# A new order of the same pieces on four engines, in a fused kernel of RWKV, a gated recurrence and two mixture-of-experts passes

## The chip, the cores and the metric

The kernel runs on one core of one Trainium2 chip. A core has five engines that each run their own list of instructions in order: TensorE (PE in the profile; PEld are its weight loads), VectorE (DVE), ScalarE (ACT), GpSimd (POOL) and SyncE (SP), which here only issues DMAs. They wait for each other through semaphores. The metric is the device time of one execution in microseconds; lower is better. Before the change it is 1342.73 us, the median of three runs (1339.48 to 1346.77).

## What is computed

The input `x` has 16 sequences of 512 tokens with 256 features. Four residual blocks follow one another, and each sees the layer-normalized rows of the one before:

```
x = x + attn_a(layernorm(x))     # RWKV: time mix with WKV scan, then channel mix
x = x + ffn(layernorm(x))        # mixture of experts
x = x + attn_b(layernorm(x))     # convolution, gates, linear recurrence, RMS norm
x = x + ffn(layernorm(x))        # mixture of experts, the same weights

# attn_a, per sequence
k, v, r = (mix of xn and its shifted rows) @ w_key, w_value, w_recept
x = x + wkv(exp(time_decay), time_first, k, v) * sigmoid(r) @ w_output
fk, fr = (mix of layernorm(x) and its shifted rows) @ f_w_key (256 x 1024), f_w_recept
x = x + sigmoid(fr) * (relu(fk) ** 2 @ f_w_value)
# attn_b, per sequence
c = depthwise_conv(x, 4 taps);  a = sigmoid(log_a) ** (8 * sigmoid(c @ W_r.T + b_r))
h[t] = a[t] * h[t-1] + sqrt(1 - a*a) * sigmoid(c @ W_i.T + b_i) * c
out = h @ W_out.T;  out = out * rsqrt(mean(out * out) + eps) * gamma
# ffn: 1024 tokens, 8 experts, 2 chosen per token
ys = gelu(x[tok] @ w1[expert]) @ w2[expert] * weight;  out[tok] += ys;  out += bias
```

The expert indices cover the first 1024 tokens, so the experts work on the rows of sequences 0 and 1, in either ffn block; the bias is added to all rows.

## The kernel before, in words

The work is cut into pieces, and each piece is a small function of the engine that runs it, named after what it does. The number in brackets is a sequence b (0 to 15), a recurrence p (0 to 15, the third block on one sequence, which is `ORDER[p]`: 2, 3, 4, 5, 6, 0, 1, 7 and so on) or an expert tile n.

- Per sequence b: norm1 (statistics `stats_in` on VectorE, a power and four row instructions `xhat` at `L580` on GpSimd), `transposes_in`, the mixes (`mixed_key`, `mixed_value`, `mixed_receptance` on VectorE, copied in part by ScalarE, `L978` and `L1032`), `keys`, `value_columns`, `recept_columns` (`L1845`), the scans of WKV on VectorE, `outputs` (`L1858`), `transposes_mid` behind norm2, and the channel mix: eight `channel_key(b, j)` (`L1851`, 6 matmuls each), eight `channel_value(b, j)` (`L1930`, 8 matmuls each) and `receptances`.
- `keep1`, `keep2`, `keep3` on GpSimd write or bring back residual rows in the ring of rows; `keep2(b)` issues a DMA that `keep1(b + 1)` waits for through the ring.
- Per recurrence p: norm3 on GpSimd and `transposes_rec`, taps of the convolution, `gate_products` (`L1851`, 24 matmuls, handed to ScalarE's `L1046`), decays on ScalarE (`L1065`, `L1069`), `recur` on VectorE, `rec_products` (`L1858`, 16 matmuls), the RMS norm and `finish`, and `residual(p)`, a DMA by GpSimd that adds the result to the rows and gives the tile back.
- Per expert tile n (128 rows of one expert, 23 tiles a pass, 46 in all): `gather(n)` (`L693`, an indirect DMA by GpSimd, for which a free buffer is needed: two buffers, so gather(n) waits for the copy of tile n − 2), `tile_in` (`L1959`, 2 matmuls), `tile_up(n, 0)` and `tile_up(n, 1)` (`L1971`, 16 matmuls each), gelu on ScalarE (`L1098`), `tile_down` (`L1979`, 16 matmuls), `rows_back` on ScalarE (`L1106`, with the store). At the end of a pass `picking(f, 0)` and `picking(f, 1)` fetch the rows of each token (`L702`, eight indirect DMAs each), and `merge(f, 0)`, `merge(f, 1)` on VectorE add them (`L3031`).

The program goes through turns −1 (`turn_first`) to 16. Turn i holds the first half of sequence i and i + 1, the channel mix of sequence i − 1, one or two recurrences from turn 4 on, and up to five expert tiles: pass 0 in turns 3 to 8, pass 1 in turns 11 to 16, none in 9 and 10. The place of a tile in its turn is a letter (`PLACES`, a to d and x), and `next_gather(i, place)` gathers the tile two behind the one of that place.

Nothing plans the order at run time. Each of the four engines has, for every turn, a function that calls its pieces one after the other; in turns 5 to 7 all four use one generic `turn(i)`. As an engine runs its list in order, a piece that waits holds back all pieces behind it on this engine, also those whose operands are there. A DMA that GpSimd issues is a piece of its list too. The lists of SyncE (loads of weights and rows, stores of the output) are written separately.

## Time and profile before

| | |
|---|---|
| median of 3 runs | 1342.73 us (1339.48 to 1346.77) |
| the profiled execution | 1340.46 us, span of its instructions 1338.7 us, granted TensorE clock 0.972 |
| TensorE busy | 1232.7 us, 92% of the span, 6044 matmuls |
| VectorE busy | 896.1 us, 67%, 1483 instructions |
| ScalarE busy | 724.6 us, 54%, 1124 instructions |
| GpSimd busy | 599.4 us, 45%, 534 instructions |
| DMA | 168.17 MB, mean 126 GB/s |

The page's second part cuts the span into 40 slices of 33.5 us. Each digit is the busy share of a slice in tenths (9 means 90% or more); PEclk is the TensorE clock that was granted, in tenths of full speed.

```profile
PE   4699989999999999999988889899999999999982
DVE  7998846557666665676878967578666665645354
ACT  3355443664735537356556657467666463553632
POOL 5335554346351442525747627367434522224014
PEclk9799999999999999999989979899999999999996
```

TensorE stands below 9 in the first two or three slices, at about 170 us, between 670 and 840 us, and at the very end. A line of a timeline reads: start, duration, engine, line, instruction, result and operands, how many instructions of one kind were run together, and in brackets the idle time of the engine before it with what ended it.

### The profile page before, as it was taken

What the parts mean: (1) busy time and instruction counts of PE and PEld (TensorE: products, weight loads), DVE (VectorE), ACT (ScalarE), POOL (GpSimd) and SP (SyncE); (2) the same over time, 40 slices, a digit from 0 to 9 for tenths busy, and PEclk for the clock granted to TensorE, in tenths of its full rate; (3) what the DMA queues carried; (4) which work ended last, traced back from release to release, by engine and by line L of the source; (5) the groups of instructions that cost most, each with busy time, mean ns of one, the idle gap of its engine ahead of it and who ended that gap; (6) DMA issues with size and microseconds to landing.
All of it is one profiled execution on the core that took longest, in us unless ns stands there. A gap on an engine that the chain in (4) does not pass through costs nothing. (4 is left out here: it accounts for less than half of the span.)

```text
span 1338.7 us, 17191 instructions
## 1 busy us (share of the span) xinstructions
PE 1232.7 (92%) x6044; PEld 998.6 (75%) x6044; DVE 896.1 (67%) x1483; ACT 724.6 (54%) x1124; POOL 599.4 (45%) x534
## 2 busy tenths in 40 slices
PE   4699989999999999999988889899999999999982
PEld 2387677887878878888766658778778788888871
DVE  7998846557666665676878967578666665645354
ACT  3355443664735537356556657467666463553632
POOL 5335554346351442525747627367434522224014
PEclk9799999999999999999989979899999999999996
DMA  7001343647365472563230023665446644554554
GB/s 213 16 25 40 86 124 105 187 124 207 102 185 149 125 205 92 149 191 118 68 94 16 17 64 119 157 164 140 128 115 163 172 146 139 179 154 131 123 162 130
DMA packets 107333, 168.17 MB, mean 126 GB/s; under 512 B 10024, under 2 KB 85296, under 8 KB 107248
## 3 DMA queue, kind: packets, MB, share of 16 engines
q1 hardware_dynamic: 88016, 120.39, 28.1%
q0 software_dynamic: 12608, 40.65, 15.3%
q10 hardware_dynamic: 6624, 6.03, 1.3%
q8 instruction: 49, 0.80, 0.2%
q14 instruction: 36, 0.29, 0.1%
HBM read 134.79 MB, written 17.06 MB: 113 GB/s over the span
## 5 line engine op out<-in xcount | busy, mean ns | idle before, releaser
L1930 PE MATMUL psum<-fwv,hid 128*128 128x256 f32 x1024 | 239.6, 383 | 0.0
L576 POOL TENSOR_TENSOR rstd<-varis,half_neg 128x4 f32<-128x4 f32 x64 | 93.8, 1465 | 309.6 <-DVE varis L2721 145.4
L1930 PEld LDWEIGHTS psum<-fwv,hid 128*128 128x128 f32 x1024 | 193.6, 193 | 27.0 <-issue 1.0
L1971 PEld LDWEIGHTS psum<-xst,ew 128*128 128x128 f32 x1472 | 178.6, 193 | 17.1 <-issue 6.5
L1971 PE MATMUL psum<-xst,ew 128*128 128x128 f32 x1472 | 181.0, 276 | 5.6 <-ACT xst L1092 3.2
L1979 PE MATMUL psum<-ew,hidt 128*128 128x256 f32 x736 | 166.9, 380 | 2.7 <-ACT hidt L1098 2.7
L1979 PEld LDWEIGHTS psum<-ew,hidt 128*128 128x128 f32 x736 | 138.8, 190 | 24.8 <-ACT hidt L1098 3.5
L580 POOL TENSOR_SCALAR xhat<-rows_ring,negmean,rstd 128x256 f32<-128x256 f32 x108 | 110.9, 1039 | 18.7 <-PE psum L1840 12.3
L1098 ACT ACTIVATE hidt<-psum 128x512 f32<-128x512 f32 x92 | 54.9, 597 | 108.3 <-PE psum L1971 108.2
L1005 ACT ACTIVATE hid<-psum 128x512 f32<-128x512 f32 x128 | 74.7, 596 | 64.6 <-PE psum L1851 44.2
L693 POOL DMA_INDIRECT xs<-xf_rows,token_of_slot x46 | 56.3, 1224 | 88.5 <-PE psum L1959 74.2
L1851 PE MATMUL psum<-xfk_hi,fwk_hi 128*128 128x512 f32 x256 | 90.3, 433 | 3.6 <-DVE parts L2742 1.7
L2915 DVE SCALAR_TENSOR_TENSOR space<-space,vec 128x512 f32<-128x512 f32 x90 | 62.1, 758 | 36.6 <-ACT space L1026 36.5
L1851 PE MATMUL psum<-parts,gw_hi 128*128 128x512 f32 x256 | 74.6, 414 | 10.6 <-ACT space L1046 10.1
L1851 PE MATMUL psum<-parts,fwk_hi 128*128 128x512 f32 x256 | 80.3, 394 | 0.0
L1851 PE MATMUL psum<-xfk_hi,fwk_lo 128*128 128x512 f32 x256 | 79.7, 393 | 0.0
L1009 ACT ACTIVATE hid<-hid 128x512 f32<-128x512 f32 x128 | 77.4, 628 | 1.6 <-ACT ys L1106 0.8
L2734 DVE SCALAR_TENSOR_TENSOR timely<-dec,vec,xn 128x512 f32<-128x512 f32 x96 | 75.4, 843 | 1.5
L1840 PE MATMUL psum<-ident,xhat 128*128 128x128 f32 x368 | 50.7, 283 | 26.0 <-POOL xhat L580 13.9
L1858 PE MATMUL psum<-wo,dec 128*128 128x256 f32 x256 | 60.7, 392 | 14.6 <-DVE dec L2862 14.6
L955 ACT ACTIVATE xn<-psum,vec 128x512 f32<-128x512 f32 x64 | 46.2, 775 | 46.7 <-PE psum L1840 43.3
L2826 DVE TENSOR_TENSOR_SCAN timely<-dec 128x512 f32<-128x512 f32 x32 | 37.6, 1216 | 50.1 <-ACT dec L991 50.1
(277 smaller groups left out, 2465.6 us busy)
## 6 DMA issues: line engine op xcount, KB each, us to landing
ew<-in_w SPq DMA_DIRECT2D x92, 1024.0 KB, 5.7
rows_ring<-bias_rows POOLq DMA_DIRECT2D x28, 512.0 KB, 5.6
rows_ring<-in_x SPq DMA_DIRECT2D x14, 512.0 KB, 4.6
rows_ring<-y POOLq DMA_DIRECT2D x14, 512.0 KB, 6.4
out<-rows_ring SPq DMA_DIRECT2D x14, 512.0 KB, 5.0
rows_ring<-space POOLq DMA_DIRECT2D x12, 512.0 KB, 4.7
ys_rows<-ys ACTq DMA_DIRECT2D x46, 128.0 KB, 4.8
xf_rows<-ew SPq DMA_DIRECT2D x2, 1024.0 KB, 4.6
```

What stands on the lines that cost most here:

```text
L576: pool.tensor_tensor(dst, src, half_neg[:, 0:src.shape[1]], ALU.pow).then_inc(done, 1)
L580: pool.tensor_scalar(dst[:, c, :], src[:, c, :], negmean[n][:, c:c + 1], rstd[n][:, col0 + c:col0 + c + 1], ALU.add, ALU.mult).then_inc(st ...
L693: pool.indirect_dma_start(out=xs[n % 2][:], out_offset=None, in_=xf_rows, in_offset=bass.IndirectOffsetOnAxis(ap=token_of_slot[:, t:t + 1] ...
L1005: nc.scalar.activation(hid[:, j % NHID, :], ring[f"f{j}"], ACT.Relu).then_inc(relu.sem, 1)
L1009: nc.scalar.activation(hid[:, j % NHID, :], hid[:, j % NHID, :], ACT.Square).then_inc(sq.sem, 1)
L1851: last = nc.tensor.matmul(dst, w[a][:, c, m * P:(m + 1) * P], src[b][:, c, :], start=n == 0, stop=n == len(terms) - 1)
L1858: last = nc.tensor.matmul(dst[:, k, :], src[:, c, k * P:(k + 1) * P], w[:, c, :], start=c == 0, stop=c == chunks - 1)
L1930: last = nc.tensor.matmul(rows4[:, k, :], hid[:, j % NHID, k * P:(k + 1) * P], fwv[:, j, :], start=j == 0 and k % 2 == 0, stop=j == FC - 1 ...
L1971: last = nc.tensor.matmul(bank_e[:, j * P:(j + 1) * P], ew1[:, c, at:at + P], xst[:, c, :], start=c == 0, stop=c == DC - 1)
L1979: last = nc.tensor.matmul(bank_e[:, 0:D], hidt[:, j, :], ew2[:, j, :], start=j == 0, stop=j == FC - 1)
L2734: nc.vector.scalar_tensor_tensor(dst[:, c, :], diff[:, c, :], col(m, c), xn[:, c, 0:T], ALU.mult, ALU.add).then_inc(st.sem, 1)
L2915: nc.vector.scalar_tensor_tensor(s.cv[:, c, :], s.xc[:, c, j:j + T], col(f"conv{j}", c), s.cv[:, c, :], ALU.mult, ALU.add).then_inc(conv.s ...
```

## The change

Every engine keeps its pieces: the same functions with the same arguments, so the same instructions, the same bytes and the same semaphores. On TensorE, ScalarE, VectorE and GpSimd the calls stand in a new order, within a turn and also across the border to the next one; the generic `turn(i)` is replaced by `turn_5`, `turn_6` and `turn_7`, each with an order of its own; computed constants are written as numbers (`7 * 16` as `112`). SyncE's list is not touched. The diff has some 3200 lines, and these are the parts that the steps below speak of. On GpSimd (`NT` is 23, so `gather(NT)` is gather(23)):

```diff
             def turn_3():
+                keep2(2)
                 gather(0)
+                keep1(3)
+                next_gather(3, "b")
                 gather(1)
-                keep2(2)
-                keep1(3)
                 norm1(4)
-                next_gather(3, "b")
                 next_gather(3, "c")
                 norm2(3)
+                keep2(3)
+                next_gather(3, "d")
+                keep1(4)
                 norm3(0)
-                next_gather(3, "d")
-                keep2(3)
-                keep1(4)
 
...
             def turn_9():
                 norm1(10)
+                mean_power(4)
                 picking(0, 0)
+                residual(4)
+                norm3(5)
                 picking(0, 1)
-                norm3(5)
-                residual(4)
                 keep2(9)
                 norm2(9)
+                gated_input(5)
                 keep1(10)
-                gated_input(5)
                 scaled_input(5)
                 norm3(6)
...
+            def turn_11():
+                keep1(11)
                 norm_power(1)
-
-            def turn_11():
                 gated_input(7)
                 scaled_input(7)
                 gather(NT)
-                keep1(11)
+                keep3(7)
                 norm1(12)
+                gather(NT + 1)
                 mean_power(7)
                 norm3(8)
-                gather(NT + 1)
+                residual(7)
                 next_gather(11, "b")
+                norm3(9)
                 next_gather(11, "c")
-                keep3(7)
-                residual(7)
-                keep2(11)
                 norm2(11)
                 gated_input(8)
+                keep2(11)
                 scaled_input(8)
-                norm3(9)
                 keep3(8)
                 keep1(12)
-                next_gather(11, "d")
                 mean_power(8)
                 residual(8)
 
             def turn_12():
                 norm1(13)
-                norm3(10)
                 next_gather(12, "b")
                 keep3(9)
-                keep3(10)
                 gated_input(9)
+                next_gather(11, "d")
+                next_gather(12, "c")
+                norm3(10)
                 scaled_input(9)
+                norm2(12)
                 keep2(12)
-                next_gather(12, "c")
-                norm2(12)
...
                 scaled_input(13)
-                keep3(13)
+                norm2(15)
+                mean_power(13)
+                next_gather(15, "c")
                 norm3(14)
 
             def turn_16():
-                mean_power(13)
                 residual(13)
-                next_gather(16, "a")
+                keep2(15)
+                next_gather(15, "d")
                 next_gather(16, "b")
                 keep3(14)
-                keep2(15)
+                next_gather(16, "a")
+                mean_power(14)
                 norm3(15)
-                mean_power(14)
                 keep3(15)
                 picking(1, 0)
```

On TensorE:

```diff
                 channel_key(2, 1)
                 channel_key(2, 2)
                 channel_key(2, 3)
+                channel_value(2, 0)
+                channel_value(2, 1)
+                channel_key(2, 4)
                 freed(ev2, 2, "e1")
                 receptances(2)
-                channel_value(2, 0)
-                channel_value(2, 1)
                 tile_in(0)
...
                 channel_value(2, 2)
+                channel_key(2, 5, -1)
                 tile_up(0, 0)
-                channel_key(2, 5, -1)
+                channel_key(2, 6, -1)
+                channel_value(2, 3)
                 tile_up(0, 1)
-                channel_value(2, 3)
+                channel_key(2, 7, -1)
                 tile_down(0)
+                channel_value(2, 4)
+                tile_in(1)
+                channel_value(2, 5)
                 freed(fr_out, 2, "s")
                 transposes_in(4)
-                channel_value(2, 4)
-                tile_in(1)
-                channel_key(2, 6, -1)
                 tile_up(1, 0)
                 freed(ev1, 4, "e1")
                 outputs(3)
+                channel_value(2, 6)
                 tile_up(1, 1)
-                channel_key(2, 7, -1)
+                channel_value(2, 7)
                 tile_down(1)
                 keys(4)
                 tile_in(2)
                 freed(zsum, 3, "z")
                 transposes_mid(3)
-                channel_value(2, 5)
                 tile_up(2, 0)
...
                 freed(ev1, 11, "e1")
                 outputs(10)
-                channel_value(9, 2)
+                channel_key(9, 6, 6)
                 channel_value(9, 3)
-                channel_value(9, 4)
                 freed(zsum, 10, "z")
                 transposes_rec(7)
+                channel_value(9, 4)
+                keys(11)
+                freed(ev3, 7, "c1")
+                transposes_mid(10)
+                channel_key(9, 7, 6)
+                freed(ev2, 10, "e1")
+                rec_products(6)
                 channel_value(9, 5)
                 channel_value(9, 6)
-                freed(ev3, 7, "c1")
-                transposes_mid(10)
                 channel_value(9, 7)
-                freed(ev2, 10, "e1")
-                rec_products(6)
-                keys(11)
                 gate_products(7, [(relu, 9, "f7"), (kvr_out, 11, "k0"), (kvr_out, 11, "k1")])
 
...
             def turn_16():
-                channel_key(15, 0)
-                channel_key(15, 1)
-                channel_key(15, 2)
-                channel_key(15, 3)
-                tile_up(41, 1)
                 freed(ev2, 15, "e1")
                 rec_products(13)
+                channel_value(14, 7)
+                tile_up(41, 0)
+                channel_key(15, 0)
+                tile_up(41, 1)
+                channel_key(15, 1)
...
                 channel_key(15, 6, 14)
                 channel_key(15, 7, 14)
+                channel_value(15, 4)
+                tile_up(43, 1)
                 channel_value(15, 5)
-                tile_up(43, 1)
+                tile_down(43)
                 channel_value(15, 6)
+                tile_in(44)
                 channel_value(15, 7)
-                tile_down(43)
                 freed(fr_out, 15, "s")
                 rec_products(14)
-                tile_in(44)
                 tile_up(44, 0)
                 tile_up(44, 1)
+                tile_down(44)
+                tile_in(45)
                 freed(fin, 14, f"f{TC - 1}")
                 transposes_rec(15)
-                tile_down(44)
-                tile_in(45)
                 tile_up(45, 0)
-                gate_products(15, [(relu, 15, f"f{j}") for j in (7, 5, 6)])
                 tile_up(45, 1)
                 tile_down(45)
+                gate_products(15, [(relu, 15, f"f{j}") for j in (7, 5, 6)])
                 freed(ev3, 15, "c1")
                 rec_products(15)
```

On VectorE:

```diff
             def turn_3():
-                experts_rows(0)
                 second_differences(2)
                 channel_mix_key(2)
                 channel_mix_high(2)
...
-                channel_mix_receptance(2)
+                weights_decayed(3)
                 weights_now(3)
-                dve.wait_ge(split_los, 2)
-                nc.vector.memset(rec_sets[0].xc[:, :, 0:3], 0.0).then_inc(cols_made, 1)
-                weights_decayed(3)
-                stats_in(4)
                 beta_sums(3)
                 decayed_values(3)
+                alpha_sums(3)
+                weighted_values(3)
+                stats_in(4)
                 denominators(3)
-                weighted_values(3)
-                alpha_sums(3)
                 numerators(3)
                 gated(3)
                 first_differences(4)
+                mixed_key(4)
                 residual_mid(3)
                 second_stats(3)
-                mixed_key(4)
...
                 denominators(9)
-                decayed_values(9)
-                gated_values(7)
-                merge(0, 0)
-                combine(7)
-                third_stats(5)
                 weighted_values(9)
-                alpha_sums(9)
                 numerators(9)
                 gated(9)
                 first_differences(10)
                 taps(5)
                 mixed_key(10)
-                mixed_value(10)
                 split_taps(5)
-                mixed_receptance(10)
                 residual_mid(9)
                 second_stats(9)
                 merge(0, 1)
+                mixed_value(10)
+                mixed_receptance(10)
                 third_stats(6)
                 weights_ahead(10)
                 scales(5)
                 second_differences(9)
                 gated_values(8)
...
                 second_differences(15)
                 channel_mix_key(15)
+                channel_mix_receptance(15)
                 channel_mix_high(15)
                 channel_mix_low(15)
                 gated_values(14)
-                recur(13)
+                mean_square(13)
                 combine(14)
+                finish(13)
                 third_stats(14)
-                mean_square(13)
-                finish(13)
-                channel_mix_receptance(15)
-                dve.wait_ge(mixture.sem, mixture.count(i, "out"))
+                dve.wait_ge(mixture.sem, mixture.count(7, "out"))
                 nc.vector.memset(rec_sets[1].xc[:, :, 0:3], 0.0).then_inc(cols_made, 1)
                 taps(14)
                 split_taps(14)
...
-                merge_bias(1)
                 mean_square(14)
                 finish(14)
                 taps(15)
                 split_taps(15)
-                gated_input(15)
                 residual(14)
                 scales(15)
+                gated_input(15)
                 scaled_input(15)
                 recur(15)
+                merge(1, 0)
                 mean_square(15)
                 finish(15)
                 residual(15)
-                merge(1, 0)
                 merge(1, 1)
 
```

On ScalarE, the end of the list:

```diff
                 gelu_of(44, 0)
                 gelu_of(44, 1)
-                conv_in(15)
                 rows_back(44)
                 tile_columns(45)
+                conv_in(15)
+                gelu_of(45, 0)
+                gelu_of(45, 1)
+                rows_back(45)
                 decay_gates_out(15)
-                gelu_of(45, 0)
                 input_gates_out(15)
-                gelu_of(45, 1)
                 nc.scalar.preload_act_table_set(LOG_EXP)
                 decays(15)
-                rows_back(45)
                 root_of(15)
                 sums_of_squares(15)
```

## Rows read from the trace of the kernel before

**Rows 1.** Windows: stretch, length, busy us (instructions) by engine, PE's granted clock, DMA share, GB/s.
```profile
0.00:67.00 67.00, 36.66 (x102) 20.35 (x103) 55.85 (x108) 24.50 (x31) 30.64 (x47) 0.90 0.42 115
...
234.00:565.00 331.00, 325.92 (x1708) 272.19 (x1707) 208.50 (x335) 179.08 (x283) 143.73 (x128) 1.00 0.52 152
...
868.00:1212.00 344.00, 338.72 (x1758) 281.30 (x1757) 219.04 (x331) 205.30 (x325) 146.87 (x130) 1.00 0.54 151
...
1277.00:1339.00 62.00, 31.96 (x163) 26.30 (x161) 28.51 (x57) 20.55 (x43) 22.40 (x23) 0.82 0.49 142
sum 1339.00, PE 1232.71 PEld 998.62 DVE 896.11 ACT 724.57 POOL 599.43; mean PE 112.06 PEld 90.78 DVE 81.46 ACT 65.87 POOL 54.49
```

**Rows 2.** TensorE's waits: engine, tile, line, releaser: us in all, times, longest.
```profile
PE psum L1840 <- POOL xhat L580: 13.9, 7, 4.4
...
PE psum L1851 <- ACT space L1046: 10.1, 4, 5.0
```

**Rows 3.** Timeline of TensorE, turns 4 and 5: start, us, engine, line, instruction, [idle before, releaser].
```profile
190.21 1.94 PE L1840 MATMUL psum<-ident,xhat 128*128 128x128 f32 x8 [4.38 <-POOL xhat L580]
...
211.56 1.04 PE L1840 MATMUL psum<-ident,xhat 128*128 128x128 f32 x8
...
233.31 0.95 PE L1840 MATMUL psum<-ident,xhat 128*128 128x128 f32 x7 [1.64 <-POOL xhat L580]
```

**Rows 4.** Timeline of VectorE, turn 3.
```profile
176.38 1.40 DVE L2714 BATCH_NORM_STATS2 stats<-rows_ring 128x6 f32<-128x256 f32 x4 [8.78 <-POOL y L580]
```

**Rows 5.** Timeline of GpSimd, turn 3.
```profile
160.34 1.19 POOL L693 DMA_INDIRECT xs<-xf_rows,token_of_slot  x1 [8.22 <-DMA xf_rows<-ew]
...
163.26 1.03 POOL L623 DMA_DIRECT2D rows_ring<-y  x1
...
180.94 9.12 POOL L580 TENSOR_SCALAR xhat<-rows_ring,negmean,rstd 128x256 f32<-128x256 f32 x4 [0.20 <-issue]
```

**Rows 6.** Timeline of GpSimd, turn 9.
```profile
649.05 1.11 POOL L702 DMA_INDIRECT ew<-ys_rows,slot_i  x1 [0.17 <-issue]
...
674.75 2.26 POOL L580 TENSOR_SCALAR hidt<-xf,negmean,rstd 128x256 f32<-128x256 f32 x4 [0.20 <-issue]
```

**Rows 7.** Timeline of TensorE, turn 9.
```profile
677.15 1.94 PE L1840 MATMUL psum<-ident,hidt 128*128 128x128 f32 x8 [5.21 <-POOL hidt L580]
```

**Rows 8.** Timeline of TensorE, turn 10.
```profile
714.77 3.07 PE L1845 MATMUL psum<-timely,wr 128*128 128x512 f32 x4 [3.16 <-ACT timely L978]
...
788.02 2.07 PE L1851 MATMUL psum<-parts,gw_hi 128*128 128x512 f32 x4 [3.11 <-ACT space L1046]
```

**Rows 9.** Timeline of GpSimd, turn 11.
```profile
841.86 0.95 POOL L693 DMA_INDIRECT xs<-xf_rows,token_of_slot  x1 [6.00 <-PE psum L1959]
...
848.95 0.89 POOL L667 DMA_DIRECT2D rows_ring<-space  x1 [5.12 <-issue]
```

**Rows 10.** Timeline of TensorE, start of turn 16.
```profile
1218.30 0.73 PE L1851 MATMUL psum<-xfk_hi,fwk_hi 128*128 128x512 f32 x2 [1.65 <-DVE parts L2742]
```

**Rows 11.** Timeline of TensorE, tail.
```profile
1276.59 3.62 PE L1858 MATMUL psum<-gwo,timely 128*128 128x256 f32 x16
...
1314.84 6.08 PE L1858 MATMUL psum<-gwo,space 128*128 128x256 f32 x16 [7.22 <-DVE space L2943]
```

**Rows 12.** Timeline of ScalarE, tail.
```profile
1307.99 0.36 ACT L1106 ACTIVATE ys<-psum 128x256 f32<-128x256 f32 x1
```

**Rows 13.** Timeline of GpSimd, tail.
```profile
1310.37 1.08 POOL L702 DMA_INDIRECT ew<-ys_rows,slot_i  x1 [25.46 <-DMA ys_rows<-ys]
...
1330.46 1.01 POOL L702 DMA_INDIRECT ew<-ys_rows,slot_i  x1 [0.30 <-issue]
```

**Rows 14.** Timeline of VectorE, tail.
```profile
1326.51 6.50 DVE L3031 SCALAR_TENSOR_TENSOR xf<-ew,choice_w,xf 128x256 f32<-128x256 f32 x14
```

**Rows 15.** Line L580: instructions, ns min/median/max, first and last start, form.
```profile
L580 POOL TENSOR_SCALAR xhat<-rows_ring,negmean,rstd x108: 546/557/5205, 75.1 to 1282.0; 128x256 f32<-128x256 f32 x108
```

**Rows 16.** Line L693 (gathers): idle time of its engine before it, by releaser.
```profile
  PE psum L1959: 74.2, 18
```

1787 lines of the change are left out of this document (1044 added, 743 removed).

## The prediction

> **What bounds the kernel now.** I read the table of windows first [rows 1]: for each stretch it gives the time in which TensorE (PE) had a matmul running. PE sums to 1232.71 of 1339 us; the next engine, VectorE (DVE), has 896. In the two long stretches with expert tiles, 675 us together, PE is idle 5.1 and 5.3 us, at granted clock 1.00. So the kernel is bound by PE's own instructions, and since the change gives every engine the same pieces, those stay. What an order can move is PE's idle time: 106.3 us, of it 30.3 before 67 us, 30.0 after 1277, 10.4 in the long stretches, and the other 35.6 in turns 2 to 4, 9 to 11 and at the end of turn 15. The view of PE's waits names who ended them [rows 2]: above all GpSimd (POOL) with the norms' rows (`L580`) and ScalarE with the gates (`L1046`). Then, stretch by stretch, I read the timelines of PE and of the engine that ended each wait.
>
> The profiled execution took 1340.46 us with a span of 1338.7, and the median of the runs is 1342.73, so 2.3 us are added at the end. A measurement of this kernel can tell about 0.5% from no change, here 6.7 us, so "same" is 1336.0 to 1349.4.
>
> **The change, place by place.** A positive number is a gain.
>
> *Head, up to 67 us.* PE waits for one serial chain of VectorE from the first load. The new order puts nothing into it and takes nothing out; it moves stats_in(1) and the routing masks into idle time beside it. Gain 0; bounds −2 (one more four-row statistics of 1.40 us [rows 4] lands in the chain, rounded up) and +1.
>
> *A, turns 2 to 4.* PE waits 4.38 us before transposes_in(4) and 1.64 us before transposes_rec(0) [rows 3]. The cause lies upstream: VectorE's statistics for norm1(4) begin at 176.38 after 8.78 us idle, released by keep1(3)'s rows on POOL (`L580`, y) [rows 4]. Those need what keep2(2)'s DMA brings, issued at 163.26, and it stood behind gather(0), which had itself waited 8.22 us for the token rows [rows 5]. The new order puts keep2(2) ahead of gather(0), so the DMA can go out at about 160.34 − 8.22 = 152, some 11 us earlier. VectorE has stats_in(4) behind weighted_values(3), and PE has transposes_in(4) after channel_value(2, 5). So both waits should go, and with the first the low clock behind it: the eight transposes took 1.94 us after the gap and 1.04 at 211.56, 0.9 more [rows 3]. That is 6.9; with the smaller waits of that stretch at most 8.5. Against it: gather(2) and gather(1) are now issued ahead of norm1(4), 1.2 us each as in [rows 5], and each can wait for PE to free its buffer. I take 6, bounds 0 and 8.5.
>
> *B, turns 5 to 8 (234:565).* 5.1 us of idle in 331 us [rows 1], in pieces of about 0.6. Each turn is now written out in an order of its own. I take 1, since a new order wins some such pieces and loses others; bounds +5 (all idle time gone) and −2 (about four new pieces).
>
> *C, turn 9.* POOL issues its 16 picks from 649.05 and only then norm3(5), whose four rows start at 674.75 and take 2.26 us [rows 6]. PE waits for it 5.21 us before transposes_rec(5), which then runs slow (1.94 for 1.04) [rows 3, 7]: 6.1 us together. Now norm3(5) stands between the two groups of eight picks, so it moves up by nearly 8 × (674.75 − 649.05)/17 = 12 us, or until its statistics from VectorE are there, and PE need not wait. The second eight picks end some 7 us later; merge(0,1), which needs them, sits in turn 10. I take 5; bounds 0 and 6.1.
>
> *D, turn 10.* (i) recept_columns(10) waits 3.16 us for the mixed value's copy on ScalarE (`L978`) [rows 8], which follows VectorE's mixing. VectorE now has mixed_value(10) and mixed_receptance(10) behind merge(0,1), 8 instructions of 6.50/14 = 0.46 us [rows 14], 3.7 us, and PE's columns of that turn wait for the last of these. I take −2.5; bounds −4 and +1. (ii) transposes_mid(10) waits for norm2(10) on POOL, the longest of that line with 4.4 us [rows 2]; the order around it hardly changes: 0. (iii) gate_products(7) waits 3.11 us for `L1046` [rows 8], which waits for residual(6)'s DMA to give back its tile. The new order puts three channel_value pieces (24 matmuls) in front; at the density of 234:565, 325.92 us for 1708 matmuls or 0.19 each [rows 1], that is 4.6 us and covers the 3.11. I take +2.5 for (ii) and (iii); bounds 0 and +7.5 (both waits).
>
> *E, turn 11.* gate_products(8) waits for `L1046`, the longest of that line with 5.0 us [rows 2]; `L1046` waits for residual(7)'s DMA to give back its tile, and that was held on POOL: gather(26) waited 6.00 us for PE, keep3(7) was issued right behind it, and residual(7) waited another 5.12 us for what keep3(7) brings [rows 9]. Now keep3(7) stands right after gather(23) and residual(7) ahead of gather(25), so the 6.00 us are no longer in this chain. The 5.0 us and a low clock of 0.9, as in A, should go. I take 6; bounds 0 and 7.
>
> *F, turns 12 to 15 (868:1212).* POOL's order changes most here: norm3(10), norm2(12) and gated_input(12) are now behind two or three gathers. PE is at work for 338.72 of 344 us [rows 1], so hardly anything is there to win: +4 at most. I take −1; the low bound −6 is one gap of the size seen in E, with its low clock.
>
> *G, end of turn 15.* channel_key(15,0) waits 1.65 us for the second norm's parts [rows 10]; rec_products(13), channel_value(14,7) and tile_up(41,0), 40 matmuls or 7.6 us, now stand in front. Gain 1.5; bounds 0 and 1.65.
>
> *H, tail.* Before, rec_products(14) (16 matmuls at 1276.59) ends at X = 1280.2 and the span at 1338.7, 58.5 us on [rows 11]. rows_back(45) stands behind decays(15) on ScalarE, at 1307.99 [rows 12]; its store lands, and the 16 picks run from 1310.37 to 1331.5, 1.34 us each [rows 13]. Beside this PE waits 7.22 us for recur(15) and then does rec_products(15) in 6.08 us, for 3.62 before [rows 11]. In the new order tiles 44 and 45 come first and gates(15) last: 98 matmuls of the tiles and 8 transposes at 0.19 us are 20 us, so rows_back(45) is at about X + 21 and the picks run from X + 23 to X + 44. But gates(15) starts only at X + 20.4, where it started at about X + 15.4, and the chain that it opens (ScalarE's gates and decays, VectorE's scan, rec_products(15), finish, residual) ran until VectorE's merges at 1326.51 [rows 14], X + 46.3. Five later is X + 51.3. Before, 12.2 us followed: 16 merging instructions, 7.4, and 4.8 for the wait for the last picks and the store. Now one of the two merges stands ahead, 3.7 are left, and of the 4.8 I keep 3 for the store: X + 58. Gain 0.5, bounds −3 (gates and the table load meet a low clock) and +4 (the old chain's own waits shrink).
>
> **Sum.** 0 + 6 + 1 + 5 − 2.5 + 2.5 + 6 − 1 + 1.5 + 0.5 = 19. Profiled: 1340.5 − 19 = 1321.5; with the 2.3 to the median: 1323.8, forecast 1324. The half widths of the bounds, added as independent errors, give about 10 us, so this case alone spans 1314 to 1334.
>
> **Rivals.**
>
> *1. The norms on POOL run slow where they now stand.* The same four rows took 2.26 us in [rows 6] and 9.12 in [rows 5]; a single row takes 546 to 5205 ns, median 557 [rows 15]. What decides is what VectorE runs beside them. If A, C and E each get a slow norm that PE waits for, each costs up to 9.12 − 2.26 = 6.9, together 20.6: 1345, no change; with two of them 1338. For it: the spread is real, and the first wait of [rows 2] is for these rows. Against: the median is the fast value, and VectorE has no more work than before. The Trainium skill ("SBUF — State Buffer", Who interferes with whom) says that VectorE and GpSimd share a pair of ports under an exclusive lock, so that one blocks the other; the spread in those rows agrees with it, and by it the price hangs on what VectorE happens to run beside a norm, which a list of pieces does not show.
>
> *2. Slower: POOL stands at a gather that comes too early.* In eight places the new order issues a gather ahead of its predecessor (2 before 1, 11 before 10, 22 before 21, 28 before 27, 31 before 30, 33 before 32, 41 before 40, 45 before 44). A gather waits until PE has copied the tile that used its buffer; such waits are 74.2 us in 18 instructions already, 4.1 each [rows 16]. Norms and gates behind it on POOL wait as well. If each of the eight adds one such wait and PE runs dry by it, it costs 8 × 4.1 = 33: 1357. It decides from (1349.4 − 1324)/8 = 3.2 us a place. Against: in the 675 us of [rows 1] with the tiles PE lost only 10.4 us, so POOL was some microseconds ahead of it there.
>
> *3. The gaps only move.* Each wait that goes brings up the next late operand a few microseconds on, and PE's idle time stays within 5 us of 106: 1338 to 1343. For: the waits of [rows 2] are many and short. Against: in A, C and E the delay has one named instruction each, and it is out of the way.
>
> **Chances.** Forecast (1314 to 1334) 0.62; better than that, with most terms at their upper bounds, 0.10; rival 1 0.14 (0.04 of it ends under 1336); rival 3 0.06 (0.02 of it under 1336); rival 2 0.08. So faster 0.62 + 0.10 + 0.04 + 0.02 = 0.78, same 0.10 + 0.04 = 0.14, slower 0.08. The range 1306 to 1340 leaves out rival 2 (0.08), about 0.07 of rivals 1 and 3, and 0.04 below.
>
> **What would show it.** In the trace of the changed kernel: no wait over 1 us before the transposes of A and C; keep3(7) and residual(7) issued well before `L1046` needs the tile, and no wait of 5 us at `L1851` (E); the wait in turn 10 at `L1845` longer than 3.16 (D); in the tail, picks issued beside the scan, and a last merge that waited for no pick (H). PE's idle time should be near 87 us (106.3 − 19). I am wrong if PE's busy sum grows by over 5 us (then the clock, not the order, decides), if the waits for `L580` grow over 20 us (rival 1), or if POOL's waits at the gathers pass 100 us with PE waiting behind them (rival 2).

## The result and the profile after

The changed kernel takes 1300.6 us (median of four runs, 1299.13 to 1306.45), the one before 1342.15 beside it: 0.9695 of its time, 95% interval 0.9654 to 0.9736, or 41.5 us less. I had forecast 1324, 18.7 us less than 1342.7, with a range from 1306 to 1340. The direction was right and the size was less than half of what came.

The profiled execution took 1301.82 us with a span of 1300.1. Its page, busy time and the 40 slices:

```profile
PE 1221.9 (94%) x6044; PEld 993.8 (76%) x6044; DVE 899.4 (69%) x1483; ACT 721.9 (56%) x1124; POOL 604.1 (46%) x534
...
PE   4699999999999999999998899999999999999982
...
PEclk9799999999999999999999999999999999999996
```

TensorE's busy time fell from 1232.7 to 1221.9 us although it does the same 6044 matmuls, and its idle time from 106 to 78 us. So of the 38.6 us between the two spans, 28 were idle time and 10.8 were matmuls that took less time. The clock accounts for most of the second part: the trace has it at its lower level, 0.50, for 75.7 us before and 53.0 after, and TensorE's busy time in these stretches is 38.9 and 23.9 us; half of the difference, 7.5 us, is my estimate of what the clock gave back. The dents of the clock in the 21st, 24th and 26th slice are gone.

The table of windows of the changed kernel, with borders at the places in TensorE's list that come nearest to those of [rows 1]:

```profile
0.00:64.30 64.30, 36.51 (x96) 20.13 (x97) 55.24 (x110) 23.69 (x30) 34.09 (x47) 0.87 0.44 119
...
154.70:221.80 67.10, 66.04 (x337) 53.83 (x335) 50.31 (x85) 31.77 (x47) 36.35 (x32) 1.00 0.56 161
221.80:558.60 336.80, 335.05 (x1756) 278.68 (x1755) 219.05 (x344) 181.10 (x292) 133.70 (x123) 1.00 0.53 151
...
639.20:683.80 44.60, 44.06 (x202) 35.84 (x201) 39.97 (x75) 32.84 (x46) 29.98 (x25) 1.00 0.36 92
683.80:764.50 80.70, 68.35 (x281) 49.89 (x279) 73.01 (x119) 52.53 (x82) 50.63 (x40) 0.98 0.14 27
764.50:852.60 88.10, 88.06 (x422) 69.90 (x423) 69.83 (x128) 61.55 (x96) 54.86 (x41) 1.00 0.56 153
...
1245.10:1300.10 55.00, 25.78 (x114) 20.93 (x114) 22.74 (x36) 17.21 (x31) 19.12 (x20) 0.75 0.47 139
sum 1300.10, PE 1221.95 PEld 993.76 DVE 899.38 ACT 721.92 POOL 604.15; mean PE 111.09 PEld 90.34 DVE 81.76 ACT 65.63 POOL 54.92
```

Windows compare stretches of time, not of work. For the rest I use another reading. At a number of places both lists of TensorE have called the same set of pieces up to there, in whatever order. The time from one such place to the next is then the time for the same work in all kernels. This table is worked out from the starts of TensorE's instructions in the profiled executions; positive is longer than before. The waits are those that the profile lists, 88.2 us in all before and 66.1 after, and each stands in the segment in whose time it falls.

```
                        before    after   waits of TensorE   my term
                            us  -before    before   after
start to end of turn 0   65.58    -1.27     30.3     27.8       0
turns 1 and 2            94.06    -3.67      2.8      0.0    \  -6 (A)
turn 3                   73.68    -6.63      6.0      1.1    /
turns 4 to 8            421.58    -4.14      5.1      2.3      -1 (B)
turn 9                   51.40    -6.77      5.4      0.5      -5 (C)
turn 10                  85.48    -4.76     14.3     12.4       0 (D)
turn 11                  98.84   -10.77      5.4      0.0      -6 (E)
turns 12 to 14          248.07    -0.21      4.8      3.4      +1 (F)
turn 15, start of 16    147.10    -2.49      3.4      1.5    -1.5 (G)
tail                     52.94    +2.08     10.7     17.1    -0.5 (H)
```

What TensorE waits for in the changed kernel:

```profile
PE psum L1977 <- POOL xhat L580: 17.6, 4, 11.3
PE psum L1995 <- DVE space L3181: 13.0, 1, 13.0
PE psum L1977 <- DVE xhat L3127: 10.1, 1, 10.1
PE psum L1982 <- ACT timely L1010: 5.6, 2, 3.7
```

The gates' line, which stood here with 10.1 us [rows 2], is gone. Of the 17.6 us for the norms 11.3 are one wait in the head, where outputs(0) had waited before.

### The profile page after: what moved, and what is told of

Same layout as the page of the kernel before. It is cut to its first block and busy times, and to the rows that moved or that the text cites. A ratio compares the mean times of both kernels' runs of the same rounds, so it can differ in the third digit from the quotient of the medians.

```text
span 1300.1 us, 17191 instructions
## 1 busy us (share of the span) xinstructions
PE 1221.9 (94%) x6044; PEld 993.8 (76%) x6044; DVE 899.4 (69%) x1483; ACT 721.9 (56%) x1124; POOL 604.1 (46%) x534
## 5 line engine op out<-in xcount | busy, mean ns | idle before, releaser
L2067 PEld LDWEIGHTS psum<-fwv,hid 128*128 128x128 f32 x1024 | 190.7, 191 | 27.9 <-ACT hid L1041 1.8
L576 POOL TENSOR_TENSOR rstd<-varis,half_neg 128x4 f32<-128x4 f32 x64 | 93.2, 1457 | 191.5 <-DVE varis L2959 100.3
L2116 PEld LDWEIGHTS psum<-ew,hidt 128*128 128x128 f32 x736 | 140.4, 191 | 26.3 <-issue 5.8
L580 POOL TENSOR_SCALAR xhat<-rows_ring,negmean,rstd 128x256 f32<-128x256 f32 x108 | 111.3, 1040 | 24.4 <-PE psum L1977 18.5
L693 POOL DMA_INDIRECT xs<-xf_rows,token_of_slot x46 | 56.2, 1221 | 115.2 <-PE psum L2096 97.6
L1977 PE MATMUL psum<-ident,xhat 128*128 128x128 f32 x368 | 49.6, 279 | 27.7 <-POOL xhat L580 17.6
L2984 DVE TENSOR_TENSOR dec<-xn 128x1024 f32<-128x1024 f32 x32 | 44.8, 1399 | 41.1 <-ACT xn L987 40.0
L1977 PEld LDWEIGHTS psum<-ident,xhat 128*128 128x128 f32 x368 | 43.6, 144 | 34.0 <-issue 19.3
L1138 ACT ACTIVATE ys<-psum 128x256 f32<-128x256 f32 x46 | 17.6, 383 | 92.9 <-PE psum L2116 92.4
```

The source lines that it names most:

```text
L576: pool.tensor_tensor(dst, src, half_neg[:, 0:src.shape[1]], ALU.pow).then_inc(done, 1)
L580: pool.tensor_scalar(dst[:, c, :], src[:, c, :], negmean[n][:, c:c + 1], rstd[n][:, col0 + c:col0 + c + 1], ALU.add, ALU.mult).then_inc(st ...
L693: pool.indirect_dma_start(out=xs[n % 2][:], out_offset=None, in_=xf_rows, in_offset=bass.IndirectOffsetOnAxis(ap=token_of_slot[:, t:t + 1] ...
L1977: last = nc.tensor.transpose(bank_t[:, c, k * P:(k + 1) * P], src[:, k, c * P:(c + 1) * P], ident[:])
L2067: last = nc.tensor.matmul(rows4[:, k, :], hid[:, j % NHID, k * P:(k + 1) * P], fwv[:, j, :], start=j == 0 and k % 2 == 0, stop=j == FC - 1 ...
L2116: last = nc.tensor.matmul(bank_e[:, 0:D], hidt[:, j, :], ew2[:, j, :], start=j == 0, stop=j == FC - 1)
```

## The experiments

Their times stand beside runs of the kernel before on the same chip. "Gained" is against before unless another kernel is named.

**Three parts of the list, and one engine.** The first three kernels take the new lists on all four engines in one part of the turns, the fourth takes GpSimd's new list alone. The new list of TensorE, ScalarE or VectorE alone, or one engine's old list among three new ones, would end in a deadlock (each engine waits for a piece that stands behind another waiting piece), so these weren't tried.

```diff
 # on GpSimd, TensorE, ScalarE and VectorE
-old lists in all turns
+e1_early:  new lists to the end of turn 8, old from turn 9
+e2_middle: new lists in turns 9 to 11
+e3_late:   new lists from turn 12 on
 # on GpSimd alone
+e4_pool:   new list in all turns
```

> All four engines have the new order from the start to the end of turn 8, and the old one from turn 9 on. Theory 1 (each place pays for itself: a wait that goes takes its idle time and the low clock behind it with it, and nothing of it is handed on): the gain is what the two profiles show for TensorE's pieces of these turns, 2.3 us before the end of turn 0, 10.6 in turns 1 to 4 and 3.9 in turns 5 to 8, together 17 us, so 1325 against 1342. Theory 2 (the places depend on each other: an engine that is early in one turn arrives early in the next, so part of the gain of the later turns comes from the order of the earlier ones): under 12 us or over 22, and the three parts don't add up to 41.5. Theory 3 (my sum): 7 us, 1335.

> All four engines have the new order in turns 9 to 11 only (TensorE up to the fourth channel_key of turn 12). Theory 1 (each place pays for itself): TensorE's pieces lose 6.8 us less in turn 9, 4.7 in turn 10, 10.8 in turn 11, together 22 us, so 1320. Theory 2 (dependence): under 17 or over 27. Theory 3 (my sum): 11 us, 1331.

> All four engines have the old order up to turn 11 and the new one from turn 12 on, with the new tail. Theory 1: what the profiles show from turn 12 on, 0.4 us or so gained in turns 12 to 14, 2 at the end of turn 15, 1.8 lost in the tail: 2 us, 1340. Theory 2 (dependence): a gain over 7 us, or a loss. Theory 3 (my sum): 1 us, 1341.

> Only GpSimd has its new list, in all turns; TensorE, ScalarE and VectorE keep theirs. In A, C and E I blamed one instruction on GpSimd's list (a DMA behind a gather, the norm behind sixteen picks, keep3 and residual behind gathers). Theory 1a (GpSimd's order is the cause there): turns 3 and 4, 9 and 11 get most of their gain, TensorE's waits before transposes_in(4), transposes_rec(5) and gate_products(8) go, 15 to 25 us gained, 1317 to 1327. Theory 1b (the lists only work together: VectorE's statistics and TensorE's place for the transposes have to move too): the waits change by under 2 us each, 0 to 8 us gained. Rival 2 of the prediction (gathers that come early stop GpSimd): slower than 1342.

Measured: e1_early 0.9923 (0.9900 to 0.9946) of before, e2_middle 0.9936 (0.9917 to 0.9955), e3_late 1.0044 (1.0031 to 1.0058), e4_pool 1.0029 (1.0018 to 1.0040). In time the three parts add up to 13 us gained, not 41: the numbers of theory 1 were missed by all three, and those of theory 2 (the places depend on each other) came true in all three. e4_pool is slower by 0.3%, where its theory 1a had 15 to 25 us gained. The segments tell why (us against before):

```
                       after  e1_early  e2_middle  e3_late  e4_pool
start to end of turn 0 -1.27     -0.37      -0.87    -1.43    -1.09
turns 1 and 2          -3.67     -1.62      +0.02     0.00    +0.04
turn 3                 -6.63     -5.54      +1.60    +1.63    -6.10
turns 4 to 8           -4.14     -0.93      +7.87    +0.16    +8.12
turn 9                 -6.77     +0.84      -6.78    +0.37    -0.31
turn 10                -4.76     +0.21      -3.77    +0.15    -2.12
turn 11               -10.77     +0.13      -3.49    +9.23    -0.30
turns 12 to 14         -0.21     +0.27      -0.19    -0.30    +3.27
turn 15, start of 16   -2.49     +0.05      +0.03    -2.53    +4.97
tail                   +2.08     -0.04      +0.58    -1.17    +0.61
```

From turn 4 on and away from the borders a segment gains nearly what it gains in the changed kernel, whatever stands before it (turn 9: −6.78 for −6.77; turn 10: −3.77 for −4.76). At a border it costs 3 (e1_early), 8 and 7 (e2_middle) and 9 us (e3_late); I take that for the cut, which falls a few microseconds earlier on one engine's list than on another's, but tried no other cut. Up to turn 3 and in the tail executions of one order differ by microseconds (turn 3 is 1.6 us longer in e2_middle and e3_late with the old order), so e1_early's smaller gain there says little. So the gains of the middle turns are local. That they also need all four lists is what e4_pool shows, for single places.

In e4_pool turn 3 has nearly its whole gain from GpSimd. In turn 11 the wait before gate_products(8) is gone, as I had said, but a new one stands in its place, 5.12 us before transposes_mid(11). The timelines of e4_pool, TensorE and then GpSimd:

```profile
859.28 1.94 PE L1872 MATMUL psum<-ident,xhat 128*128 128x128 f32 x8 [5.12 <-POOL xhat L580]
```
```profile
831.42 0.88 POOL L667 DMA_DIRECT2D rows_ring<-space  x1
...
847.23 1.94 POOL L576 TENSOR_TENSOR rstd<-varis,half_neg 128x4 f32<-128x4 f32 x1 [13.06 <-DVE varis L2753]
```

residual(7) goes out at 831.42 (it was 848.95 [rows 9]), but norm3(9) (the power at `L576` below, then its rows) now stands ahead of norm2(11) and waits 13.06 us for statistics that VectorE's old list makes late. And rival 2's mechanism is there as well: where gather(11) goes ahead of gather(10), TensorE waits for the tile of the latter, and the same at tile 42 with 3.23 us:

```profile
376.60 0.69 PE L1991 MATMUL psum<-ident,xs 128*128 128x128 f32 x2 [3.68 <-DMA xs<-xf_rows,token_of_slot]
```

**Three moves on GpSimd.**

```diff
 turn 3:   +keep2(2)        ahead of gather(0)      -behind gather(1)
 turn 9:   +norm3(5)        behind picking(0, 0)    -behind picking(0, 1)
 turn 11:  +keep3(7)        behind gather(23)       -behind gather(26)
           +residual(7)     ahead of gather(25)     -behind keep3(7)
```

> The kernel before with three moves on GpSimd alone: keep2(2) ahead of gather(0); norm3(5) between the two groups of eight picks; keep3(7) right after gather(23) and residual(7) ahead of gather(25). With GpSimd's whole new list the first move gave all of turn 3's gain (6.1 us), but norm3(9), which stands ahead of norm2(11) in that list, made a new wait of 5.12 us in turn 11. Theory 1 (one named instruction a place): turn 3 gives 6, turn 11 gives the wait of 5.0 and the low clock behind it, 7 in all, since norm3(9) stays where it was; turn 9 gives 0 to 1, because norm3(5)'s statistics come late from VectorE and its four rows ran 7.05 us there; together 13 to 14 us, 1327 to 1328. Theory 2 (the lists only work together): turn 11 gives under 2, together 6 to 8, 1333 to 1335.

Measured: 0.9909 (0.9889 to 0.9928), 12 us gained. Turn 11 gained 7.55, where theory 1 had 7, and turn 9 1.44, where it had up to 1. Turn 3 gained 3.66 instead of 6, and the stretch before it lost 3.22, with VectorE idle for 3.65 us near 146 us and TensorE waiting 4.17 us before channel_key(2, 0), where it had waited 0.95. The clock behind that wait was low; the windows are of this run and of the kernel before:

```profile
160.95 1.19 PE L1889 MATMUL psum<-xfk_hi,fwk_hi 128*128 128x512 f32 x2 [4.17 <-issue]
```
```profile
161.00:164.00 3.00, 3.00 (x7) 2.42 (x8) 3.00 (x4) 0.12 (x1) 1.84 (x1) 0.50 0.25 20
```
```profile
161.00:164.00 3.00, 3.00 (x15) 2.42 (x14) 3.00 (x5) 1.91 (x4) 2.69 (x3) 1.00 0.70 206
```

Up to there this run has the old order. s3_turn9_all, below, has it in turn 3 too and shows the same wait of 4.17 us (3.26 us lost), so I take it for a variation between executions. It blurs what the first move is worth in time: turn 3 is 3.66 us shorter than before, but only 1.94 shorter than in s3_turn9_all. The wait itself is clear: before transposes_in(4) TensorE waits 4.38 us in the kernel before, 1.63 in s3_turn9_all, and not at all here. In turn 11 (GpSimd, then TensorE):

```profile
831.16 0.98 POOL L667 DMA_DIRECT2D rows_ring<-space  x1
```
```profile
841.48 1.18 PE L1889 MATMUL psum<-parts,gw_hi 128*128 128x512 f32 x4
```

The gates start with no idle time ahead, and their first four matmuls take 1.18 us, where those of gate_products(7) took 2.07 behind a wait [rows 8]. Step E was right in its cause.

**Turn 9.**

```diff
 TensorE:  +tile_down(22)   ahead of value_columns(9)    -behind it
           +channel_key(8, 5) ahead of channel_value(8, 2)
 ScalarE:  +rows_back(22)   ahead of values_out(9)       -behind it
 GpSimd, in s3_turn9_all only:
           +norm3(5)        behind picking(0, 0)         -behind picking(0, 1)
```

> The kernel before with two moves on TensorE and one on ScalarE, none on GpSimd: tile_down(22) ahead of value_columns(9), channel_key(8,5) ahead of channel_value(8,2) (so ahead of transposes_rec(5)), and rows_back(22) ahead of values_out(9). From the end of tile_down(22) to the transposes it takes 30.7 us before and 30.5 after the change, by the chain picks, merge(0,0), third_stats(5), norm3(5); what changed is how much work TensorE has in between: 3.4 and 1.4 us more. Theory 1: these two moves are what turn 9's gain of 6.8 comes from, not GpSimd's order: the wait of 5.2 us falls to 0.5 or so and the low clock behind it goes, 6 us gained, 1336. Theory 2 (my step C: norm3(5) behind the sixteen picks is the cause): the wait stays over 3 us, under 3 us gained, 1339 or more.

> The kernel before with the two moves on TensorE and the one on ScalarE in turn 9, and norm3(5) between the two groups of eight picks. In the run without the last, norm3(5) waited for the sixteenth pick until 676.6 though its statistics were ready at 669.9, and TensorE still waited 1.4 us for it, after 1.2 before channel_key(8,5). Theory 1 (both parts are needed, and enough): the wait before the transposes goes, and the segment gains 5.5 to 6.8 us. Theory 2 (something else in the new lists is needed): under 5.

Measured: s2_turn9 0.998 (0.9964 to 0.9996), turn 9 3.90 us shorter and turns 4 to 8 1.18 longer; s3_turn9_all 0.9977 (0.9962 to 0.9991), turn 9 4.70 shorter. s2_turn9 lies between its theories: the wait before the transposes fell from 5.21 to 1.36 us, and a new one of 1.18 came before channel_key(8, 5). s3_turn9_all stays under the 5 of its theory 2, so something else in the new lists is needed. Of the 1.18 us by which turns 4 to 8 are longer in s2_turn9, 0.95 come from the edit itself, as tile_down(22) now waits 0.79. TensorE's two moves, with ScalarE's, bring more than GpSimd's order (3.9 and 1.4 in s1_three_moves), and together they fall 2.07 us short of 6.77. About half of that (1.05) is at gate_products(5), with a wait of 0.70 us before it; 0.65 are a longer wait for norm3(5), and most of the rest is before channel_key(8, 5). norm3(5)'s four rows in s3_turn9_all, and in the changed kernel:

```profile
668.76 7.06 POOL L580 TENSOR_SCALAR hidt<-xf,negmean,rstd 128x256 f32<-128x256 f32 x4 [0.20 <-issue]
```
```profile
653.59 4.21 POOL L580 TENSOR_SCALAR hidt<-xf,negmean,rstd 128x256 f32<-128x256 f32 x4 [0.20 <-issue]
```

7.06 against 4.21 us for the same instructions, and TensorE waits for them 1.19 us in the one and 0.54 in the other. Which of the other moves take these away was not tried.

**The gathers' order.**

```diff
 GpSimd, the changed kernel's list:
-gather 0, 2, 1, ..., 11, 10, ..., 22, 21, ..., 28, 27, ..., 31, 30, ..., 33, 32, ..., 41, 40, ..., 45, 44
+gather 0, 1, 2, ..., 45, in the places where gathers stand
```

> The changed kernel, with the gathers in ascending order in the places where gathers stand (eight pairs exchanged back), all else new. Theory 1: the reversed pairs neither help nor hurt when the other engines have their new lists, as TensorE has no wait of a microsecond for a gather there: 1300.6, within 2 us. Rival 2 of the prediction: each reversed pair costs, so this is faster by over 4 us. Rival 3: the reversals are part of what pays (the gather that would wait longer lets the norm behind it through), so this is slower by over 4 us.

Measured: 0.9683 (0.9665 to 0.9701) of before, 1299.3 us, no difference from 1300.6 that these runs can tell. By segments, two of the eight pairs do something: with gather(1) ahead of gather(2) turn 3 is 2.6 us longer, and with gather(10) ahead of gather(11) the wait of 1.72 us before keys(6) is gone (1.6 us less in turns 4 to 8).

**What a wait costs.**

```diff
 TensorE, the changed kernel's list; each call moved up, so that it waits for its norm:
+transposes_mid(6)  ahead of tile_down(13)      +transposes_mid(7)  ahead of tile_up(17, 1)
+transposes_mid(13) ahead of channel_value(12, 6)
+transposes_in(15)  ahead of tile_up(34, 1)     +transposes_mid(14) ahead of tile_down(35)
```

> The changed kernel with five groups of transposes called earlier on TensorE, so that each has to wait for its norm in a stretch where TensorE had no idle time: by the profile of the changed kernel the waits should be about 2.0 us (transposes_mid(6)), 4.3 (transposes_mid(7)), 1.4 (transposes_mid(13)), 2.0 (transposes_in(15)) and 6.4 (transposes_mid(14)), 16 us in all. This measures what a wait costs besides its own length. Theory 1: after a wait of 3 us or more the granted clock stands at its lower level for several microseconds of work, 2.5 us or more lost on top of each; the short ones cost their length only: 16 + 5 = 21 us, 1322. Theory 2 (what I had put down, 0.9 us for a gap): 16 + 4.5, spread over all. Theory 3: the norms end later too or earlier because the pieces in between moved, so the waits are less than half of that.

Measured: 1326.9 us, 0.989 of before and 26.3 us more than the changed kernel. The waits came as expected (1.95, 4.31, 1.34, 1.90 and 5.60 us, with small ones behind them 18.5 in all), and the segments grew by 27.6. Theory 1 was right in kind and low in size, 9.1 us on top instead of 5, and wrong in that the wait of 1.95 us cost about twice its length, though the one of 1.90 did not:

```
wait (with small ones behind it)       us of waits   segments grew by   on top
transposes_mid(13)                         1.7             1.9            0.2
transposes_mid(6)                          2.4             4.6            2.1
transposes_mid(7)                          5.0             8.3            3.3
transposes_in(15)                          3.1             3.8            0.7
transposes_mid(14)                         6.3             9.0            2.7
```

The two waits of nearly the same length, before transposes_mid(6) and transposes_in(15). The trace has the clock at 0.50 for 3.4 us behind the first, and at 1.00 all through the second, whose transposes run at full rate:

```profile
446.43 1.78 PE L1977 MATMUL psum<-ident,xhat 128*128 128x128 f32 x8 [1.95 <-POOL xhat L580]
```
```profile
1071.62 1.06 PE L1977 MATMUL psum<-ident,xhat 128*128 128x128 f32 x8 [1.90 <-POOL xhat L580]
```

So the length of a short wait does not tell alone whether the clock falls; what else decides was not tried. TensorE after the wait of 4.31 us, and the granted clock (seventh column of figures) in that stretch:

```profile
532.71 1.94 PE L1977 MATMUL psum<-ident,xhat 128*128 128x128 f32 x8 [4.31 <-POOL xhat L580]
534.44 3.62 PE L2108 MATMUL psum<-xst,ew 128*128 128x128 f32 x16
537.85 4.06 PE L1982 MATMUL psum<-timely,wk 128*128 128x512 f32 x8
```
```profile
522.00:528.00 6.00, 6.00 (x37) 5.51 (x36) 2.90 (x8) 2.08 (x4) 0.98 (x1) 1.00 0.00 1
...
532.50:536.00 3.50, 3.29 (x16) 3.33 (x17) 1.02 (x1) 0.00 (x0) 3.33 (x3) 0.50 0.00 0
536.00:540.00 4.00, 4.00 (x14) 2.80 (x14) 2.63 (x4) 1.09 (x2) 1.11 (x1) 0.65 0.39 57
540.00:544.00 4.00, 4.00 (x16) 2.76 (x15) 0.00 (x0) 0.00 (x0) 0.00 (x0) 1.00 0.59 242
```

The transposes take 1.94 us for 1.04, and the 16 matmuls of the tile behind them, which run in 1.95 elsewhere, 3.62: it is not only the first group that is slow. The clock stands at 0.50 (1.2 GHz) and is back at 1.00 (2.4 GHz) some 6 us after the work has begun again. The Trainium skill ("TensorE: Matmul & The Clock Gate", Part 1) has these two levels in its table of states, full rate when warm and half rate when cold.

**A norm alone.**

```diff
 VectorE, the changed kernel's list:
 second_stats(10)
+wait until norm2(10)'s four rows are done
 ...
 second_stats(12)
+wait until norm2(12)'s four rows are done
```

> The changed kernel, in which VectorE waits after second_stats(10) and after second_stats(12) until GpSimd has done the four rows of norm2(10) and norm2(12), so that those rows run with VectorE idle. In the changed kernel they took 5.78 and 6.25 us beside VectorE's mixing, and TensorE waits 2.57 and 3.17 us for them. Theory 1 (rival 1's mechanism: what VectorE runs beside a norm sets how long it takes): the four rows take 2.2 to 2.3 us each and both waits of TensorE go to under 0.5; the time falls by up to 5 us where VectorE's own delay (2 to 3 us at each place) is not waited for, 1297, or stays where it is. Theory 2: the rows stay at 5 us or more with VectorE idle, and the slow ones have another cause.

The rows of norm2(10) and norm2(12), in the changed kernel and with VectorE waiting:

```profile
738.79 5.78 POOL L580 TENSOR_SCALAR xhat<-y,negmean,rstd 128x256 f32<-128x256 f32 x4 [0.20 <-issue]
```
```profile
896.85 6.25 POOL L580 TENSOR_SCALAR xhat<-y,negmean,rstd 128x256 f32<-128x256 f32 x4 [0.49 <-issue]
```
```profile
740.65 2.16 POOL L580 TENSOR_SCALAR xhat<-y,negmean,rstd 128x256 f32<-128x256 f32 x4 [0.20 <-issue]
```
```profile
901.74 2.17 POOL L580 TENSOR_SCALAR xhat<-y,negmean,rstd 128x256 f32<-128x256 f32 x4 [0.49 <-issue]
```

5.78 and 6.25 us become 2.16 and 2.17: the mechanism of rival 1 is shown. In time it gave nothing, 1301.4 us: turns 12 to 14 gained 2.9 us on the changed kernel, and turn 10 lost 2.2, because VectorE's mixing came later and TensorE now waited 5.65 us before keys(11), where it had waited 2.08. (Turns 12 to 14 got a new wait too, 2.30 us before rec_products(9).) The Trainium skill ("SBUF — State Buffer", Who interferes with whom) has the two engines lock each other out of a shared port pair; both runs agree with that, in that the one gets faster when the other waits.

**A mix moved back, and the tail.**

```diff
 VectorE:  +mixed_value(10), mixed_receptance(10) ahead of merge(0, 1)
 GpSimd:   +norm3(15) ahead of mean_power(14)
 ScalarE:  +conv_in(15) ahead of rows_back(44)     +rows_back(45) ahead of decays(15)
 TensorE:  +transposes_rec(15) ahead of tile_down(44)
           +gate_products(15) ahead of tile_down(45)
```

> The changed kernel with two edits far apart. (a) VectorE does mixed_value(10) and mixed_receptance(10) ahead of merge(0,1) again. Theory 1: recept_columns(10), which waits 3.70 us, then waits less by the 3.7 us of the merge: turn 10 gains 2.5 to 3.7. Rival: the wait is set by something else (ScalarE's copies, TensorE's own early arrival) and changes by under 1 us. (b) In the tail norm3(15) stands ahead of mean_power(14) on GpSimd, conv_in(15) ahead of rows_back(44) and rows_back(45) ahead of decays(15) on ScalarE, transposes_rec(15) ahead of tile_down(44) and gate_products(15) ahead of tile_down(45) on TensorE. Theory 1: the end is set by the chain that gate_products(15) opens (37.1 us from its start to the end); it starts 7 us earlier, and then the picks are last: 3.7 us gained. Rival: the picks set the end already, and this costs 3 us or more, as they start later. Together 1294 by theory 1, 1303 by the rivals.

Measured: 1302.5 us, no gain on 1300.6; both parts went the rivals' way in kind, the second without the 3 us that its rival had put down as lost. recept_columns(10) waits 3.49 us instead of 3.70, so the merge was never what it waits for: the wait is for ScalarE (`L1010`, the copies of keys and values), whatever VectorE does. And in the tail gate_products(15) did start at 1257.7 instead of 1263.0, but transposes_rec(15) came early enough to wait 3.13 us, and the picks, which started 3.7 us later, were now last: VectorE waits 3.25 us for the last of them.

**Two mixtures.**

```diff
 n1_mixed, the changed kernel's lists with:
+gathers in ascending order except 2 ahead of 1      +old tail on all engines from tile_down(44) on
 n2_gathers_norm, the changed kernel's lists with:
+the same gathers      +VectorE waits behind second_stats(12) for norm2(12)'s rows
```

> The changed kernel with the gathers in ascending order except 2 before 1 (with all in order, keys(6) lost its wait of 1.7 us, 2.1 in all, and turn 3 got 2.6 slower), and with the old tail on all engines from tile_down(44) on (the new one cost 2.1 us more in this kernel's segments from the second tile_up of tile 44 on). Theory 1 (both add up): 1296 to 1297. Rival: the tail depends on how TensorE arrives there, and it stays within 1.5 us of 1300.

> The changed kernel with the gathers in ascending order except 2 before 1, and VectorE waiting after second_stats(12) for norm2(12)'s rows (not in turn 10, where that wait cost 3.0 us because keys(11) came late). Theory 1 (single segments add up): 2.1 + 2.5 + 0.4 = 5 us under the changed kernel, 1295 to 1296. Rival (an engine that is early in one segment waits in the next): 1299 or more.

Measured: n1_mixed 1303.2, so the old tail is no better: with the wait that it brings (transposes_rec(15), 3.13 us) it ends 61.4 us after rec_products(14), and the new one 56.0 to 60.3 us after it in the six executions that have it. n2_gathers_norm 1298.05 us, 0.966 of before (0.9634 to 0.9685); its segments show 1.8 us in turns 4 to 8 and 2.9 in turns 12 to 14 under the changed kernel, but the turns up to 2, which have the same order, were 3.3 us longer in its profiled execution. Its interval overlaps that of the changed kernel, so it isn't shown to be faster.

## Why the prediction was right in direction and wrong in size

Two steps failed above all. The low clock behind a gap was priced at 0.9 us, and the waits outside the named places were put at nothing or left to cancel, in turns 1 and 2 and in B. A third was smaller: D (i) put down a loss of 2.5 us that came as 0.5.

*What bounds the kernel* was right: no engine but TensorE comes near, and all of the gain is TensorE's idle time and clock. But the sentence that an order can move idle time and nothing else was wrong. 10.8 of the 38.6 us are busy time.

*The low clock* is a term that was mis-sized. In turns 3, 9, 10 and 11 the waits shrink by 17.1 us and the time by 28.9. I took the first eight transposes behind the gap, 1.94 for 1.04, and put 0.9 us down for a gap, in A, C and E, 2.7 in all. w1_five_waits has 9.1 us for 18.5 us of waits, 2.1 to 3.3 us for each of the three behind which the clock fell. It could have been read from the kernel before: a window over 788 to 797 us shows a clock of 0.50, and so does one over 854 to 858, many groups behind the gap:

```profile
788.00:797.00 9.00, 8.15 (x12) 4.01 (x13) 7.93 (x24) 7.08 (x9) 4.44 (x2) 0.50 0.15 29
854.00:858.00 4.00, 3.69 (x11) 3.12 (x12) 0.00 (x0) 2.11 (x5) 0.88 (x2) 0.50 0.82 212
```

With 2.5 us in place of 0.9 for each of the gaps of A, C and E, and one such gap in D, the sum is 19 + 4.8 + 2.5 = 26 us.

*A* (6 forecast, 10.3 measured in turns 1 to 3). The step was right: with keep2(2)'s move and no other in turn 3 the wait before transposes_in(4) is gone (s1_three_moves), and GpSimd's list alone gives 6.1 of turn 3's 6.6 us (e4_pool). What I had counted only in the upper bound as "the smaller waits of that stretch" were those before transposes_mid(2) and channel_key(2, 0), 1.54 and 0.95 us, which went too; turns 1 and 2 are 3.7 us shorter. These two vary: s1_three_moves waits 4.17 us at the second with the order of before.

*B* (1 forecast, 4.1 measured). I let wins and losses cancel in turns 4 to 8. The waits there were of one kind, 0.57 to 0.69 us at an expert tile for ScalarE's copy or gelu, repeated in three equal turns; the new lists put other work between, and each such segment is 0.7 to 0.9 us shorter. Only keys(6), 1.72 us, and transposes_mid(8), 0.53, came as new waits.

*C* (5 forecast, 6.8 measured). Nearly the right number, by luck, for the wrong reason. The chain from tile_down(22) over picks, merge(0,0), third_stats(5) and norm3(5) takes 30.7 us before and 30.5 after; my step put the end of it down to norm3(5)'s place, which is worth 1.4. I had not asked whether norm3(5)'s statistics are there any earlier: VectorE makes them from the merged rows. TensorE's list, which has 4.8 us more work between the two ends of the chain, pays more (3.9 us in s2_turn9).

*D* (0 forecast, 4.8 measured). Step (i) failed: I held the mix behind merge(0,1) for what recept_columns(10) waits for, where the profile names ScalarE's copies. It cost 0.5 us instead of 2.5. (iii) was right and gave the wait of 3.11 us before gate_products(7), and the low clock behind it. (ii) gave nothing, as forecast: the wait for norm2(10) fell from 4.35 to 2.57 us, and keys(11) got one of 2.08. No run takes turn 10's moves apart.

*E* (6 forecast, 10.8 measured). Right in cause, shown by s1_three_moves (7.55). The rest I put down to the end of the gap in turn 10, whose low clock reached into turn 11, where value_columns(11) took 6.49 us (3.67 now). In the changed kernel, GpSimd and TensorE:

```profile
778.28 0.97 POOL L644 DMA_DIRECT2D rows_ring<-bias_rows  x1
...
799.70 0.89 POOL L667 DMA_DIRECT2D rows_ring<-space  x1
```
```profile
812.52 1.18 PE L1988 MATMUL psum<-parts,gw_hi 128*128 128x512 f32 x4
```

*F* and *G* (−1 and 1.5 forecast, 0.2 and 2.5 measured) were right within their bounds: F gives back 3.1 us at transposes_mid(12) and wins them in the other turns.

*H* (0.5 forecast, −2.1 in the profiled execution). The picks moved beside the scan and the last merge waited for none, as I wrote. One execution can't price this term: six have the new tail on all engines (the changed kernel, e3_late, g1_in_order, w1_five_waits, p1_norm_alone, n2_gathers_norm), and in them the tail lasts 50.7 to 55.0 us, 52.8 in the mean, for 52.9 before. So the term was right within what can be told. From the end of rec_products(14) to gate_products(15) it takes 20.0 to 23.2 us, where I had 20.4. What varies is above all tile_down(45): in the changed kernel's execution it waits 2.29 us for its weights (a DMA into `ew`) and the clock falls behind it; in w1_five_waits it waits 0.69 us for the gelu and takes 3.72 us. TensorE at the end of the changed kernel:

```profile
1257.97 5.38 PE L2116 MATMUL psum<-ew,hidt 128*128 128x256 f32 x16 [2.29 <-DMA ew<-in_w]
...
1281.99 5.99 PE L1995 MATMUL psum<-gwo,space 128*128 128x256 f32 x16 [13.04 <-DVE space L3181]
```

Of what I had said the profile would show, most is there: no wait before the transposes of A, 0.54 us before that of C, no wait at the gates, 3.70 for 3.16 us at `L1982` (the old `L1845`) in turn 10. TensorE's idle time is 78 us, not 87. None of the three signs of being wrong came: the busy sum fell, the waits for `L580` are 18.1 us in all, and GpSimd's waits at the gathers, 97.6 us, stay under 100.

*Rival 1* was right as a mechanism (p1_norm_alone), and it holds 3.2 us at norm2(12) and 2.6 at norm2(10), but not at the places I had named. *Rival 2* is seen in e4_pool, where the other three lists are old (3.68 and 3.23 us); beside the new lists two of eight pairs matter, in opposite directions. *Rival 3*, that waits only move, is what GpSimd's list alone does in turn 11; the four lists together don't.

Sum of the misses between the two profiled executions: 38.6 − 19 = 19.6 us, of it about 8 of busy time (10.8 − 2.7) and 11.5 of idle time, most of that in turns 1 and 2, B and D (i). How the 19.6 divide is read from one pair of executions, of which the first turns and the tail vary by a few microseconds.
